# A fused decoder layer on one core: smaller first input groups, per-column vectors loaded as rows, and side work spread over more steps of the recurrence

## The reference, cut to what matters

```python
def _L0_attn_ref(x, ln_g, ln_b, w_qkvb, b_qkvb, w_out, b_out):
    ...
    normed = (x - mu) * lax.rsqrt(var + LN_EPS) * ln_g + ln_b
    proj = normed @ w_qkvb + b_qkvb
    q, k, v, beta_pre = jnp.split(proj, 4, axis=-1)
    beta = jax.nn.sigmoid(beta_pre)
    ...
    k = k / jnp.maximum(jnp.linalg.norm(k, axis=-1, keepdims=True), NORM_EPS)
    def step(S, inp):
        q_t, k_t, v_t, beta_t = inp
        retrieval = jnp.einsum('bhij,bhj->bhi', S, k_t)
        S = S + jnp.einsum('bhi,bhj->bhij', beta_t * (v_t - retrieval), k_t)
        o_t = jnp.einsum('bhij,bhj->bhi', S, q_t)
        return (S, o_t)
    ...
    return x + scan_out @ w_out + b_out
...
x = x + _L0_attn_ref(_layernorm(x), ...)      # delta-rule recurrence, 16 heads of 16
x = x + _L0_xattn_ref(_layernorm(x), ctx_1024, ctx_1024, mask, ...)
x = x + _L0_ffn_ref(_layernorm(x), ...)       # int8 activations, ternary weights w1, w2
return x
```

## Time and profile before

| | before |
|---|---|
| median of 3 runs | 1118.63 us (1118.08 to 1118.74) |
| the profiled execution | 1113.54 us, its span 1111.8 us |
| PE busy | 929.6 us, 84% |
| DVE busy | 922.3 us, 83% |
| ACT busy | 653.0 us, 59% |
| POOL busy | 479.2 us, 43% |
| mean granted clock of PE | 0.919 of full |

### The profile page before, as it was taken

The page is one execution under the profiler, slowest core; times in us unless marked ns, Lnnn a source line. Parts: engine busy times, 40 slices in busy tenths (PEclk is TensorE's granted clock), DMA queues, the critical chain, the costliest instruction groups (busy, mean ns, idle before and its releaser), DMA issues.

```text
span 1111.8 us, 19572 instructions
## 1 busy us (share of the span) xinstructions
PE 929.6 (84%) x6107; PEld 706.9 (64%) x6114; DVE 922.3 (83%) x2749; ACT 653.0 (59%) x1592; POOL 479.2 (43%) x667
## 2 busy tenths in 40 slices
PE   8788899999999999999999989899797610696066
PEld 7466777877877878778778777666565410343044
DVE  5876789999999999999999998666665879699887
ACT  3477565666566666666666653546576432596085
POOL 4424354464453553644535533315466560690000
PEclk9689999999999999999999999999998955699579
DMA  9800000000300000000000000214200000000012
GB/s 144 136 1 6 7 9 7 7 11 7 119 11 7 9 8 6 11 7 6 11 6 9 9 5 10 87 58 139 88 1 0 1 0 0 1 1 1 0 58 95
DMA packets 30149, 30.49 MB, mean 27 GB/s; under 512 B 7136, under 2 KB 25440, under 8 KB 30048
## 3 DMA queue, kind: packets, MB, share of 16 engines
q1 hardware_dynamic: 28128, 29.12, 10.8%
q10 hardware_dynamic: 1920, 0.14, 0.2%
HBM read 20.85 MB, written 4.19 MB: 23 GB/s over the span
## 4 chain that ended last, share of the span: by engine, by line
PE 65%; DVE 23%; issue 6%; ACT 3%; POOL 1%; DMA 1%; SPq 1%; DVEq 0%; ACTq 0%; POOLq 0%
PE ps L1789 6%; PE ps L1797 6%; PE ps L1728 5%; PE psG L1751 5%; PE psY L1765 4%; PE psX L1765 4%; PE ps L1909 4%; PE psY L1930 3%; PE psY L1843 3%; PE psG L1745 2%; PE psX L1843 2%; PE psX L1930 2%; PE ps L1857 2%; PE ps L2087 2%; PE psG L1909 2%
## 5 line engine op out<-in xcount | busy, mean ns | idle before, releaser
L517 POOL TENSOR_TENSOR arena<-arena 128x256 f32<-128x256 f32 x32 | 23.4, 730 | 304.9 <-DVE arena L1095 301.7
L622 ACT ACTIVATE arena<-ps 128x512 f32<-128x512 f32 x128 | 72.9, 596 | 47.3 <-PE ps L1789 47.0
L1789 PE MATMUL ps<-work 32*128 32x256 f32 x512 | 93.5, 407 | 2.4 <-ACT work L668 2.3
L485 POOL TENSOR_SCALAR_AFFINE_SELECT arena<-arena 128x2048 f32<-128x2048 f32 x32 | 92.2, 2882 | 2.2
L587 ACT ACTIVATE arena<-ps,nparity 32x256 f32<-32x256 f32 x124 | 51.2, 458 | 48.1 <-PE ps L1728 47.7
L1751 PE MATMUL psG<-arena 128*128 128x512 f32 x128 | 73.6, 658 | 1.7 <-DVE arena L1161 1.7
L1789 PEld LDWEIGHTS ps<-work 32*128 32x128 f32 x512 | 62.0, 187 | 19.3 <-issue 12.9
L1106 DVE TENSOR_TENSOR arena<-arena 128x256 f32<-128x256 f32 (+1 forms) x96 | 66.5, 692 | 3.3
L1109 DVE TENSOR_REDUCE arena<-arena 128x64 f32<-128x256 f32 (+1 forms) x96 | 65.9, 686 | 3.3
L1728 PE MATMUL ps<-work,arena 128*128 128x64 f32 x496 | 62.2, 281 | 6.9 <-DVE work L1121 6.8
L1765 PEld LDWEIGHTS psY<-work,arena 128*128 128x128 f32 x512 | 59.5, 194 | 13.0 <-DVE arena L1178 12.4
(11 more groups left out here) (332 smaller groups left out, 2632.1 us busy)
## 6 DMA issues: line engine op xcount, KB each, us to landing
arena<-in_mask_BxSxS_ik SPq DMA_DIRECT2D x8, 1024.0 KB, 7.0
xs<-arena SPq DMA_DIRECT2D x256, 16.0 KB, 1.8
arena<-in_ctx SPq DMA_DIRECT2D x8, 512.0 KB, 4.1
out<-xs SPq DMA_DIRECT2D x32, 128.0 KB, 1.7
arena<-in_x SPq DMA_DIRECT2D x8, 384.0 KB, 21.8
arena<-in_L_ffn_w SPq DMA_DIRECT2D x2, 1024.0 KB, 24.2
arena<-in_L_attn_w_qkvb SPq DMA_DIRECT2D x2, 512.0 KB, 5.2
arena<-in_x SPq DMA_DIRECT2D x8, 96.0 KB, 7.2
```

What stands on the lines that cost most here:

```text
L485: G.affine_select(out=pairs, in_=pairs, compare_op=ALU.is_ge, fill=0.0, base=0, pattern=[[0, NH], [-CT, B], [0, CT]], channel_multiplier=1 ...
L622: A.activation(attn[j % 2][:, r * 512:(r + 1) * 512], ps[(2, 0)[r % 2]][:, :], ACT.Copy).then_inc(att_out, 1)
L1789: last = M.matmul(ps[(2, 0)[r % 2]][:, f * 2 * P:(f + 1) * 2 * P], kq[j % 4][rows, f * P:(f + 1) * P], qe[rows, f].rearrange("p e t -> p ( ...
```

## The change

It has seven parts.

1. The groups of x are (0,2), (2,8), (8,14), (14,32). DVE takes the third group's statistics too, ahead of `keys_normed(0)`, and finishes its factors in pieces between the products and scales of chunk 0. SP loads that group ahead of `wo_s` and `bb_s`.
2. ACT's input moments are of 18 columns, two in each of the slots 0 to 8; DVE makes their factors in step 8 (`late_inputs`).
3. The other side work moves back: `weights_summed` to slots 9 and 10, `ternary_sums` and `ternary_factors` to step 11, `weights_rounded` and `bounded_weights` to slots 12 to 15 with two pieces each, `weights_ternary` to slots 16 to 19 with two each, the two context loads to step 21.
4. ln_g, ln_b and the biases are loaded by three DMAs as 12 rows of 128; PE turns them, DVE copies them to `columns`.
5. For the first group DVE writes the two variances into PSUM, adds `floors` and `ones` as tensors, and seeds from there. The seed is one instruction in place of two, here and in every other inverse root that uses it.
6. PE multiplies `ones` 30 times, into psX.
7. In step 0 PE no longer has `far_gram(1, 0)` and `norms_turned(2)` between the parts of the attention; they stand behind them, the second behind `queries(3)`; `values(1)` stands ahead of `keys(3)`. On DVE `key_norms(0)` goes ahead of `parity`, and `key_norms(2)` and `near_products(1)` go into `solve(0)` at t = 1 and t = 8.

```diff
-X_GROUPS = [(0, 2), (2, 8), (8, NCK)]
+X_GROUPS = [(0, 2), (2, 8), (8, 14), (14, NCK)]
+MOMENT_SLOTS = 9
...
-                if j == 10:
+                if j == 21:
                     sp.wait_ge(tern_ready, 8)
...
-                first = 8 * (k + 1)
+                first = X_GROUPS[3][0] + 2 * k
                 if k == 0:
-                    act.wait_ge(x_in[2], 16 * B)
-                for i in range(first, first + 8):
+                    act.wait_ge(x_in[3], 16 * B)
+                for i in range(first, first + 2):
...
-                if j < 3:
+                if j < MOMENT_SLOTS:
                     input_moments(j)
-                elif j < 5:
...
+                elif 12 <= j < 16:
+                    for p in range(2 * (j - 12), 2 * (j - 12) + 2):
                         weights_rounded(p)
...
+            for k, vec in enumerate((ln_g, ln_b, b_qkvb)):
+                act.dma_start(vector_rows[DC * k:DC * k + vec.shape[0] // P, :],
+                              vec.rearrange("(c p) -> c p", p=P)).then_inc(vec_in, 16)
...
-                own(V.tensor_scalar(dst.bitcast(I32), t.bitcast(I32), 1, None, ALU.logical_shift_right))
-                own(V.tensor_scalar(dst.bitcast(I32), dst.bitcast(I32), -1.0, SEED, ALU.mult, ALU.add))
+                own(V.tensor_scalar(dst.bitcast(I32), t.bitcast(I32), -0.5, SEED, ALU.mult, ALU.add))
...
+                if k == 0:
+                    return psY[:, 0:4].rearrange("p (e n) -> p e n", e=2)
...
+            def late_inputs():
+                v.wait_ge(x_sums, 5 * MOMENT_SLOTS)
+                total, squares = columns_of(3, mean, rstd)
+                input_seed(3, squares)
+                for _ in range(3):
+                    input_step(3)
+                input_factors(3, total, 1.0)
...
+            v.wait_ge(vec_T, 1)
+            V.tensor_copy(columns[:, :], ps[2][:, 0:6 * DC]).then_inc(vec_ready, 1)
...
-                    solve(0, {4: ((keys_normed, 1), (far_products, 1), (key_norms, 2)), 12: ((keys_normed, 2),)})
+                    solve(0, {1: ((key_norms, 2),), 4: ((keys_normed, 1), (far_products, 1)), 8: ((near_products, 1),),
+                              12: ((keys_normed, 2),)})
...
-                if j == 0:
-                    near_products(1)
...
-                    if j == 2:
-                        v.wait_ge(x_sums, 3 * 17)
-                        input_factors(8, NCK, mean[:, 8:NCK], 1.0, rstd[:, 8:NCK])
+                    if j == MOMENT_SLOTS - 1:
+                        late_inputs()
...
-            for _ in range(42):
-                M.matmul(psY[:, 0:P], ones[:, :], ones[:, :], start=True, stop=True)
+            for _ in range(30):
+                M.matmul(psX[:, 0:P], ones[:, :], ones[:, :], start=True, stop=True)
...
+            pe.wait_ge(vec_in, 48)
+            M.transpose(ps[2][:, 0:6 * DC], vector_rows, ident[0:6 * DC, 0:6 * DC]).then_inc(vec_T, 1)
```

158 lines of the change are left out of this document (100 added, 58 removed).

## The result

| | before | changed |
|---|---|---|
| median of 4 runs each | 1118.36 us (1113.21 to 1118.74) | 1089.83 us (1087.54 to 1093.50) |
| the profiled execution | 1113.54 us, span 1111.8 us | 1093.50 us, span 1091.6 us |
| mean granted clock of PE | 0.919 | 0.921 |

The ratio of the runs is 0.9758 (95% interval 0.9717 to 0.98). The forecast of the span was 1092.2 and the span is 1091.6. The medians differ by 28.5 us, not by 19.6, and the new median lies 1.2 us under the low end of the range.

The account below looks back on a forecast made before the run. The loop was taken as bound by PE and DVE, early steps held above a 20.2 us pace by ACT's long slots. Terms 0.4 + 8.4 + 13.4 - 3.0 + 0.4 = 19.6 us took 1118.6 to 1099.0; range 1091 to 1107.

Parts of the forecast that it names:

- Up to `start_chunk(0)`: Start of the kernel, before 36.72 us: 1.1 gained on DVE's chain, less 0.1 for late factors and 0.6 for PE's clock.
- Rival (e): First group's variances in PSUM still wait for POOL: 3.4 us back, total stays 1099; shares chance 0.50 with the main forecast.
- The load term: Removing twelve vector loads moves the second x group's load at 14.96 by 0 to 2.2 us; taken as 0.
- Step 0: From 36.72 to 71.84: 35.1 us falls to 26.7, including 1.5 for late keys and 1.0 for PE's clock.
- rival (b): x comes late, third group holding `keys_normed(0)` or fourth holding ACT's slot 0; 1105 with 3 us each; chance 0.12.
- Steps 1 to 9: From 71.84 to 262.14: 190.3 us falls to 173.0 plus 3.9, as two-column slots fit ACT's room of 2.48.
- Rival (c): Early slots have less room than slot 9, since moments wait for each other: 0.4 in nine slots, 1102.6; chance 0.15.
- (d): Slower: side work in ACT's slots ahead of `outputs_turned` lies fully on the path, 32.7 worse, 1131.7; chance 0.03.
- rival (a): Early steps nearer the pace: full clock in step 0 and after, slot 10 covered, second x group earlier; 1094.4; chance 0.20.
- Steps 10 to 20: Moved side work in the loop: slots 9 and 10 over the room, ternary factors 0.4, bounded weights 0.9; 3.0 lost.
- After the loop: Behind the loop: thirteen inverse roots lose one 0.2 us instruction each, mostly not on the bound; 0.4 gained.
- Carrying the 5.1 over: Whole kernel: runs' median 1118.63 is 5.1 above the profiled 1113.54, and this difference was assumed to stay.

## Why the prediction was right, point by point

The change is faster, for the reason given: the early steps came to the pace. The size is another matter. The span met its forecast within 0.6 us, and that is luck in part: the tail gave 6.0 us more than forecast, while the start, step 0 and the last two steps gave 0.7, 1.9 and 3.4 less. The median came 9.2 us below its forecast.

**What bounds it** held. The pace of 20.2 us is there in every trace, and the first steps came to it.

**Up to `start_chunk(0)`, 0.4 gained.** By the profiled pair it is 0.3 lost (36.99 against 36.72), by ten traces with the three row loads 0.4 gained (34.77 to 37.24, mean 36.3). The variances took 0.24 us as forecast:

```profile
6.08 0.24 DVE L1073 SCALAR_TENSOR_TENSOR psY<-tmp,floors 128x2 f32<-128x2 f32 x2
```

The same sums from SBUF to SBUF by `TENSOR_SCALAR` took 3.43 to 3.70 in the four traces that have them, both forms while POOL writes its zeros. In all four they began at 5.64 to 5.91 and ended at 9.33 or 9.34, just behind POOL's last large zero (8.77 to 9.30 in the kernel before), which ties the wait to POOL's writes. The form has changed with the place, so the runs don't tell which of the two did it. The Trainium skill (SBUF — State Buffer, "Who interferes with whom") says that a DVE instruction with two SBUF inputs contends with GpSimd where that reads SBUF, not where it only writes; the 0.24, with two inputs in SBUF beside POOL's writes, agrees. What the prediction took from there on instructions with one input is not borne out by the row it names: that instruction has one input and waited, and the trace doesn't tell in which mode it ran. Rival (e) is out. The load term was taken at 0 of 0 to 2.2 and is wrong: in the four traces with twelve loads the second group's statistics start at 14.77, 14.96, 15.28 and 15.40, in the ten with three at 12.42 to 14.45, mean 13.3. That is 1.8 us. My reason, that the stream ran as fast later without them, said nothing on the first microseconds. The move of the parity and the shift, forecast at 1.1, gave 0.7: from the second group's statistics to `keys_normed(0)` it is 11.1 us instead of 11.8, since the third group's statistics and what follows them took 3.6 instead of 3.2 and filled the hole. PE's low clock, sized at 0.6 with 1.7 as the bound, then ate it: DVE waits 2.02 for `far_gram` at 31.80. The fall itself came as the prediction read it from the kernel before's windows; whether 42 matmuls of ones would have kept the clock was not tried alone.

**Step 0, 8.4 gained.** The addition of step 0 came at 51.53 (51 forecast), that of step 1 at 76.20 (74). From `start_chunk(0)` to `start_chunk(1)` it took 65.61 - 36.99 = 28.6 us against 26.7 forecast; 6.5 gained. `solve(0)` took 14.5 of the 14.9 forecast. `state(0)` began 2.7 us behind the addition, where it is 0.9 at the pace: 1.9 against the 1.5 I took for the keys. The rest, 2.9, is the low clock, for which I took 1.0 with 2 as the bound:

```profile
54.27 3.51 PE L1787 MATMUL ps<-work,arena 128*128 128x64 f32 x16
```

is the state's 16 matmuls in step 0, which last 1.90 to 2.00 at full clock, and the granted clock is 0.50 from 54 to 60 us. The new wait of ACT for x did not happen: behind the fourth part of the attention ACT went on at once, since all of x was there by 43:

```profile
43.21 0.41 ACT L700 ACTIVATE scrap<-arena 128x256 bf16<-128x256 f32 x1
...
46.96 0.62 ACT L648 ACTIVATE work<-ps,columns 128x128 f32<-128x128 f32 x2 [1.49 <-PE ps L1856]
```

The slot is over before PE is, so the idle time stands behind it. Of rival (b) nothing was seen. Which part of the change makes this gain the forecast had left open. The runs say that either the short slot or the new order is nearly enough: the step takes 25.7 us with the short slot in the old order, 24.2 with six columns in the new order, 23.7 to 24.8 with both, and 32.2 in the kernel before.

**Steps 1 to 9, 13.4 gained.** Steps 2 to 8 ran at 20.2, step 8 to 9 was 23.23 with 23.3 forecast. From `start_chunk(1)` at 65.61 to the addition of step 9 at 242.00 it took 176.4 us, where the forecast had 173.0 + 3.9 and the kernel before 190.3: 13.9 gained. The mechanism was as said, but the room of 2.48 was not the room: 4.4 us is, by the run with three slots. Rival (c), 0.4 in each of nine slots, is out, for the distances from 3 to 8 stand at 20.17 to 20.22, and with it (d). Of rival (a) the earlier second group and the covered slot 10 came true, full clock in step 0 did not, and the two steps behind it were still 0.8 and 0.3 us over the pace.

**Steps 10 to 20, 3.0 lost.** Step 9 to 10 took 1.9 over the pace, the next two 0.8 and 0.6, the rest nothing: 3.2. The size is right, its cause is not. I put 1.7 down to slots 9 and 10 and 0.9 to the bounded weights, which cost nothing; the run without the Newton steps shows 1.4 of the 1.9 to be PE's clock behind its wait for the late factors, and slots 9 and 10 lie within the room of 4.4. Only the 0.4 of the ternary factors was where I put it (20.62 in step 11 of that run).

**After the loop, 0.4 gained.** This is the term that was mis-sized. The tail gave 6.4 us in the profiled pair, and the seeds together are worth 6.5 (4.0 to 9.0) and 3.3 us (0.7 to 5.9) by the medians' jobs. Counting instructions at 0.2 was wrong by a factor of about ten, because it left out PE's clock, with which the length of the tail goes. There are also twelve roots and not thirteen, one of them in the last step of the loop. With 3.3 to 6.5 in place of 0.4 the sum is 22 to 26. The differences of the medians in three jobs are 28.5, 28.2 and 23.4, with 95% intervals of 4 to 5 us to either side. So the seeds explain some 3 to 6 of the 9 us by which the forecast of the difference was short; the rest is not placed. In which of the places it arises was not settled; the ten in cross attention give 1.0 (-1.7 to 4.0) by the medians, and a tail longer than any of the ten with one instruction.

**Not forecast at all: the last two steps.** They took 42.5 us against 39.1 (41.1 and 42.6 in the other two traces of the changed kernel, 38.0 in the other of the kernel before). DVE does the norms of the second block there, PE waits, and its clock falls sooner or later. PE in the changed kernel and in the one with the keys earlier:

```profile
650.13 3.67 PE L1787 MATMUL ps<-work,arena 128*128 128x64 f32 x16 [2.43 <-DVE work L1161]
...
672.00 2.25 PE L1787 MATMUL ps<-work,arena 128*128 128x64 f32 x16 [1.73 <-DVE work L1161]
```

```profile
646.03 2.00 PE L1786 MATMUL ps<-work,arena 128*128 128x64 f32 x16 [2.43 <-DVE work L1161]
...
666.09 2.00 PE L1786 MATMUL ps<-work,arena 128*128 128x64 f32 x16 [1.33 <-DVE work L1161]
```

The first wait is the same 2.43 us, and the matmuls behind it run slow in one and at full speed in the other. The clock fell in both, but not at the same moment. The changed kernel first, then the other:

```profile
649.00:650.00 1.00, 0.00 (x0) 0.00 (x0) 0.93 (x3) 0.00 (x0) 0.59 (x1) 0.85 0.00 0
650.00:651.00 1.00, 0.87 (x4) 0.87 (x5) 1.00 (x2) 0.00 (x0) 1.00 (x2) 0.50 0.00 0
```

```profile
647.00:648.00 1.00, 1.00 (x11) 1.00 (x11) 0.77 (x3) 0.00 (x0) 1.00 (x1) 1.00 0.00 0
649.00:650.00 1.00, 1.00 (x2) 0.34 (x1) 0.45 (x1) 0.98 (x3) 1.00 (x1) 0.50 0.11 27
```

In one it fell at the end of the wait, in the other past 648, behind the sixteen matmuls, and the step took 20.06 instead of 21.87.

**Carrying the 5.1 over** from profile to median was the last weak step. The kernel before's runs reach from 1108.1 to 1121.4 within one job of 23, far more than the 0.2% that the prediction gave a measurement; a single profiled execution stands anywhere in that. The spans differ by 20.2, the medians by 28.5, because one profile fell on the fast side of its kernel and the other on the slow side of its own.

## What to carry to other kernels

Side work in front of moves that feed another engine is to be cut until each piece fits the room; with short pieces the order of the work around them hardly mattered here. The idle time behind a piece that keeps the pace is a safe lower bound for the room (2.48 us here). The room itself is the length of a piece that is too long, less the wait that it causes on the other engine (4.4 us, from two pieces). A term that makes PE wait two microseconds at once is to be priced with the slow matmuls behind it, not by its own instructions: 2.5 us of small instructions cost 3.9. Where identical programs spread over 1%, one profile against another can place a difference but not size it, and a 4 us difference of a stretch needs the same stretch in several executions.
